# Attention and expert layer on one core: order of row maxima, low parts and pair products changed

## What is computed

```python
xn = _layernorm(x)
# attention: one head of 128, all 2048 keys for each query
qkv = xn @ w_qkv.T;  q, k, v = split(qkv)
probs = softmax((q @ k.T) * scale)             # needs the largest score of each row
attn = (probs @ v) reshaped @ w_proj.T + b_proj
# experts: 8 of them, each row goes to its best 2
h = xn @ W_in + b_in
route = top2 of softmax(h @ W_gate + b_gate), renormalised
mid = relu(h @ W1[e] + b1[e]);  eout = mid @ W2[e] + b2[e]
moe = (sum over e of route * eout) @ W_out + b_out
return x + attn + moe
```

## Time and profile before

| | us |
|---|---|
| median of 3 runs | 266.45 (265.16 to 271.34) |
| the profiled execution | 266.31 |
| its span, first to last instruction | 264.5 |
| TensorE busy | 233.3 (88%) |
| VectorE busy | 147.9 (56%) |
| GpSimd busy | 142.2 (54%) |
| ScalarE busy | 119.0 (45%) |
| mean granted clock of TensorE | 0.974 |

### The profile page before, as it was taken

How to read it: one execution, slowest core, us unless ns; L and a number is a source line. 1 busy time by engine, 2 the same in 40 slices (tenths; PEclk the granted TensorE clock), 3 DMA queues, 4 the chain that set the end, 5 groups by cost and what they waited for, 6 DMA issues and landing times.

```text
span 264.5 us, 4573 instructions
## 1 busy us (share of the span) xinstructions
PE 233.3 (88%) x1590; PEld 211.6 (80%) x1590; DVE 147.9 (56%) x340; ACT 119.0 (45%) x275; POOL 142.2 (54%) x163
## 2 busy tenths in 40 slices
PE   8898695978898888979999999999999489888994
PEld 8797594766686666779999999999988278788993
DVE  5945756277517867353545454545576535785462
ACT  1644240240264444733454545454477426546461
POOL 4029005888888810014666665656068888888300
PEclk9999898999999999999999999999999959999999
DMA  6799700111111021001222222222111113112011
GB/s 198 310 309 332 196 2 30 41 40 42 40 40 41 30 72 30 0 10 32 74 68 74 68 72 72 71 71 61 36 36 42 46 45 71 40 42 69 22 40 41
DMA packets 23047, 19.53 MB, mean 74 GB/s; under 512 B 3280, under 2 KB 19696, under 8 KB 22768
## 3 DMA queue, kind: packets, MB, share of 16 engines
q1 hardware_dynamic: 20000, 14.71, 18.5%
q0 software_dynamic: 2048, 4.20, 5.8%
q10 hardware_dynamic: 976, 0.33, 0.5%
HBM read 10.97 MB, written 8.26 MB: 73 GB/s over the span
## 4 chain that ended last, share of the span: by engine, by line
PE 67%; DVE 12%; POOL 6%; ACT 5%; issue 5%; DMA 3%; ACTq 1%; POOLq 0%; DVEq 0%
PE ps L1037 13%; PE ps L1023 13%; DVE part_max L598 7%; PE ps L848 5%; POOL wtab L380 5%; PE ps L789 4%; PE ps L791 4%; PE ps L790 4%; PE ps L910 3%; PE ps L797 3%; PE ps L923 3%; PE ps L919 3%; PE ps L920 3%; DMA w_raw<-in_L_attn_w_proj_dram 2%; ACT pf L455 2%
## 5 line engine op out<-in xcount | busy, mean ns | idle before, releaser
L343 POOL COPY wst<-wtab 128x1156 f32 x39 | 45.0, 1153 | 51.3 <-DVE y_sb L735 51.2
L608 DVE TENSOR_TENSOR pl<-pf,ph 128x512 fp32r<-128x512 f32 x48 | 35.2, 733 | 34.4 <-ACT pf L455 33.4
L455 ACT ACTIVATE pf<-ps 128x512 f32<-128x512 f32 x64 | 38.0, 594 | 28.9 <-PE ps L791 21.7
L454 ACT ACTIVATE ph<-ps 128x512 fp32r<-128x512 f32 x48 | 28.7, 599 | 38.6 <-PE ps L791 35.7
L598 DVE TENSOR_REDUCE part_max<-ps 128x1 f32<-128x1024 f32 x32 | 38.8, 1219 | 10.9 <-PE ps L848 8.6
L353 POOL DMA_INDIRECT slots_in<-hl,slots x32 | 32.8, 1024 | 21.8 <-DVE slots L674 14.8
L1037 PE MATMUL ps<-wst,mid 128*128 128x128 f32 x312 | 41.3, 275 | 0.9 <-DVE x_sb L625 0.9
L380 POOL DMA_INDIRECT wtab<-slots_out,slots x32 | 33.0, 1031 | 16.1 <-DMA slots_out<-y_sb 8.4
L1023 PE MATMUL ps<-xgT,wst 128*128 128x128 f32 x312 | 41.3, 275 | 0.0
L727 DVE TENSOR_SCALAR mid<-ps,wst 128x128 f32<-128x128 f32 x78 | 23.7, 346 | 28.9 <-PE ps L1023 28.9
L1037 PEld LDWEIGHTS ps<-wst,mid 128*128 128x128 f32 x312 | 38.0, 192 | 1.1 <-issue 1.0
(11 more groups left out here) (145 smaller groups left out, 359.0 us busy)
## 6 DMA issues: line engine op xcount, KB each, us to landing
wtab<-in_L_ffn_W_dram SPq DMA_DIRECT2D x16, 256.0 KB, 6.2
xg<-slots_in SPq DMA_DIRECT2D x39, 64.0 KB, 2.0
slots_out<-y_sb SPq DMA_DIRECT2D x39, 64.0 KB, 1.5
slots_in<-wst SPq DMA_DIRECT2D x2, 1024.0 KB, 5.0
x_sb<-in_L_attn_x_dram SPq DMA_DIRECT2D x4, 256.0 KB, 4.9
out_dram<-x_sb SPq DMA_DIRECT2D x3, 256.0 KB
wtab<-in_L_ffn_b_dram SPq DMA_DIRECT2D x1, 512.0 KB, 7.4
slots_in<-hl,slots POOLq DMA_INDIRECT x32
```

The costliest lines, as they stand in the source:

```text
L343: pool.tensor_copy(wst[:, t % 4, :], wtab[:, bass.ds(experts[t], 1), :].rearrange("p a n -> p (a n)")).then_inc(Z["staged"], 1)
L455: act.activation(pf[:, i % 3, :], ps[:, st_bank(i), :], ACT.Exp).then_inc(Z["pf_done"], 1)
L608: dve.tensor_tensor(pl[:, i % 3, :], pf[:, i % 3, :], raw(ph[:, i % 3, :]), ALU.subtract).then_inc(Z["lo_done"], 1)
```

## The change

The groups, the tiles and all instructions stay; what changes is their order on TensorE and VectorE.

1. VectorE takes the maxima of a step (and `row_max`) ahead of the step's low part, where it took them behind it.
2. Where a step has two pairs, TensorE makes the second behind `values`, where both stood ahead of it. If a step has one, it stays where it was.
3. The prefix product is issued in step 1 of the first group, not in step 3.
4. `PAIR_STEP` is spread anew for the second, third and fifth row: `[1, 2, 2, 3, 3, 4, 4, 5]` becomes `[1, 2, 2, 3, 4, 4, 5, 6]`, `[1, 2, 4, 5, 7, 8, 10, 11]` becomes `[1, 3, 5, 7, 9, 11, 12, 13]`, and `[1, 2, 3, 4]` becomes `[1, 2, 4, 5]`.
5. The second block of the experts' output is transposed at step 22 of phase two, not 21, and multiplied at 23. The counts that a transpose and a pair wait for are computed from the tables; they come to the same blocks and pairs as before.

```diff
-    PAIR_STEP = [[4, 5, 5, 6], [1, 2, 2, 3, 3, 4, 4, 5], [1, 2, 4, 5, 7, 8, 10, 11], [1, 4, 7, 10], [1, 2, 3, 4], []]
+    PAIR_STEP = [[4, 5, 5, 6], [1, 2, 2, 3, 4, 4, 5, 6], [1, 3, 5, 7, 9, 11, 12, 13], [1, 4, 7, 10], [1, 2, 4, 5], []]
...
-    BLOCK_AT = {12: 0, 21: 1, 25: 2}
+    BLOCK_AT = {12: 0, 22: 1, 25: 2}
...
             for g in range(PRE):
                 for k in range(STEPS[g]):
-                    if FIRST[g] + k >= PLAIN:
-                        low(FIRST[g] + k)
                     for m in pairs_at(g, k):
                         pair_max(g + 1, m)
                     if k == PAIR_STEP[g][-1]:
                         row_max(g + 1)
+                    if FIRST[g] + k >= PLAIN:
+                        low(FIRST[g] + k)
...
-                    low(i)
                     for m in pairs_at(g, k):
                         pair_max(g + 1, m)
                     if g + 1 < NG and k == PAIR_STEP[g][-1]:
                         row_max(g + 1)
+                    low(i)
...
-                for m in pairs_at(g, k):
-                    if m == 0:
-                        pe.wait_ge(Z["q_hi_ready"], g + 2)
-                    if g > PRE:
-                        pe.wait_ge(Z["moe_added"], 1)
-                    pair(g + 1, m)
+                for m in pairs_at(g, k)[:1]:
+                    step_pair(g, k, m)
+
+            def step_pair(g, k, m):
+
+                if m == 0:
+                    pe.wait_ge(Z["q_hi_ready"], g + 2)
+                blocks = sum(at < FIRST[g] + k - BASE_B for at in BLOCK_AT)
+                if g >= PRE and blocks > 0:
+                    pe.wait_ge(Z["moe_added"], blocks)
+                pair(g + 1, m)
...
-                    if g == 0 and k == 3:
+                    if g == 0 and k == 1:
                         prefix()
                     beside(g, k)
                     if i >= 2:
                         values(i - 2)
+                    for m in pairs_at(g, k)[1:]:
+                        step_pair(g, k, m)
```

More of the change, by code:

```diff
@@ L1061, in _, with moe_transpose @@
                 layer2(t)
-            def moe_transpose(b):
+            def moe_transpose(b, pairs):
                 pe.wait_ge(Z["c_ready"], TB * (b + 1))
-                if b == 0:
-                    pe.wait_ge(Z["max_read"], FIRST_PAIR[PRE + 2])
-                else:
-                    pe.wait_ge(Z["max_read"], FIRST_PAIR[NG])
+                pe.wait_ge(Z["max_read"], pairs)
                 for j in range(TB):
@@ L1092, in _ @@
                     if s in BLOCK_AT:
-                        moe_transpose(BLOCK_AT[s])
+                        moe_transpose(BLOCK_AT[s], FIRST_PAIR[g + 1] + sum(at <= k for at in PAIR_STEP[g]))
                     if s - 1 in BLOCK_AT:
@@ L1101, in _ @@
             values(LAST - 1)
-            moe_transpose(NR - 1)
+            moe_transpose(NR - 1, FIRST_PAIR[NG])
             for r in range(ROUNDS[NG - 1]):
```

## The result

| | before | after |
|---|---|---|
| median of the runs compared | 268.89 (265.16 to 271.36, 4) | 254.43 (253.91 to 255.89, 4) |
| profiled execution | 266.31 | 253.91 |
| its span | 264.5 | 252.2 |
| TensorE busy | 233.3 (88%) | 230.7 (91%) |
| mean granted clock | 0.974 | 0.986 |

The ratio is 0.957, 95% interval 0.951 to 0.963: faster. Forecast were 254.1 us, in a range of 251.0 to 258.8. Two of the four runs of the kernel before, 271.34 and 271.36, count as slow ones and are left out of the ratio, which therefore stands for some 11 us and not for the over 14 between the two medians. In the other comparisons its median was 266.3 to 266.7 us.

A forecast was written before the change was run, and what follows sets the result against it. Outside the expert stage, TensorE's pair matmuls waiting for VectorE's maxima (11 waits) were taken as the bound. Gains of 3.2 + 1.3 + 5.7 + 2.0 = 12.2 us off 266.31 gave 254.1 us, range 251.0 to 258.8.

The forecast's parts named there:

- Third group's stage: 75.11 to 109.20: four waits for maxima, costing 6.1 us with restarts, shrink to 0.4; gain 5.7 us (4.5 to 6.1).
- First group's stage: 39.51 to 50.18: earlier prefix product frees the maxima, gain 3.2 us (1.5 to 3.3), half of it a lower clock disappearing.
- Second group's stage: 53.94 to 75.11: the chain of eight maxima stays the bound; row product at 71.95, not 73.28, gain 1.3 us (0.5 to 1.6).
- The first maximum stays at 55.83: Second group's stage: its first maximum keeps its place, held by the query copy and the expert table.
- Expert stage: 109.20 to 189.00: untouched by the change, only starts earlier, near 99, with 4.6 us reserve before the first loaded rows.
- Behind it: Behind the expert stage: nothing until step 12, then the fifth group's waits of 2.7 us shrink to 0.6; gain 2.0 (1.0 to 2.6).
- first rival: The clock: idle pieces bring the lower level, 257.5 us, or shorter idle avoids it behind, 250.7; chance 0.12.
- The rule weighed: GpSimd table copies hold only low parts, never maxima, so 254.1 us stands; if maxima too, 1.4 us lost, 255.5.
- The low part as the late one: Third and fifth groups' stages: values wait for late low parts in every pair step, 14.6 us, 268.7 us; chance 0.04.
- no wait gone: Each wait moves to the next pair because reductions bound; only the prefix's 3.2 us remain, 263.1 us; chance 0.06.
- a gather as the gate: Behind step 12 GpSimd's gather sets the pace and the last 2.0 us go, 256.1 us; scatter or gather chance 0.08.
- clock rival: Lower clock in two stretches, 1.7 us each, 257.5 us; or at most 3.4 won between 207.70 and 224.08, 250.7; chance 0.12.

The follow-up runs named there:

- e1: The changed kernel with VectorE taking the low part of a step ahead of its maxima again, on the new table; 260.36 us, ratio 0.980.
- e5: The kernel before with one edit alone, maxima ahead of low parts in every step; 258.88 us, ratio 0.973.
- e6: The kernel before with one edit alone, the prefix product at step 1 of the first group; 263.93 us, ratio 0.994.
- e4: The changed kernel with the old tables, so pairs at their old steps and second block transposed at step 21; 256.53 us, ratio 0.961.
- e3: The changed kernel with both pairs of a step ahead of values again; 255.80 us, ratio 0.961.
- e11: e8 with GpSimd's four table copies behind scatters 6, 9, 12 and 15 instead of 20, 23, 26 and 29, without warming; 254.24 us, ratio 0.958.
- e8: The changed kernel with the expert table and gates taken in the first group's last step, not ahead of the second group's first maximum; 255.17 us, ratio 0.960.
- e2: The changed kernel with the prefix product back in step 3 of the first group; 257.26 us, ratio 0.967.
- e10: The changed kernel plus ten unread matmuls to keep TensorE warm in the wait before step 12's transposes; 253.96 us, ratio 0.956.
- e13: e12 with the first pair of the first group's steps one step earlier, at 3, 4, 5, 6; 251.71 us, ratio 0.948.
- e7: The changed kernel plus 30 unread matmuls to keep TensorE warm in the wait before step 12's transposes; 256.80 us, ratio 0.968.
- e12: e11 plus ten unread matmuls to keep TensorE warm in the wait before step 12's transposes; 252.39 us, ratio 0.950.

## Why the prediction was right

The time was right to 0.3 us, and the sum to 0.2 (12.2 forecast, 12.4 between the profiled executions). Not all of its terms were. The order of work accounts for some 9.9 of the 12.4: 1.7 in the first group's stage, 0.8 in the second, 5.4 in the third and 2.0 behind the expert stage. The other 2.5 are 1.6 and 1.2 us that the execution of before lost at the lower clock, less the 0.35 by which the changed kernel's first pair came later. The mechanism was right and gave four fifths of the forecast; that the sum came out to 0.2 is luck.

**Third group's stage: forecast 5.7, measured 5.39.** The mechanism is shown (e1, e5). The runs also separate what the prediction put together:

| first row product of the stage to expert transpose | low part first | maxima first |
|---|---|---|
| old table | 36.18 (before), 36.15 (e6) | 32.81 (e5, e4) |
| new table | 34.17 (e1) | 30.79 (after, e3) |

Order gives 3.4 with either table, the table 2.0 with either order; they add up, though the table's 2.0 are not the same waits: with low parts first they are two of the four stalls (e1 keeps 2.1 of 5.0), with maxima first the two waits behind held low parts that e4 shows. The 0.3 us between forecast and measurement is in the size of a stall. The forecast took 6.1 us for four of them, 0.28 each on top of the 5.0 of the rows, and let 0.4 stay. The 0.4 was right (0.3 at steps 12 and 13, above), so the four had cost 5.7, 0.17 each on top of the rows. e1 has 0.2: its piece is 3.4 longer with 2.7 in three waits.

**First group's stage: forecast 3.2, measured 3.35, and here the term was right by luck.** The step that failed is "half of this is the clock ... I take it as gone". The clock did go, but the change did not do it: e5 has the late prefix and the same idle pieces (1.47 and 1.32 us), and ran at 1.00 in 10.00 us. What the edit is worth is 10.00 - 8.29 = 1.7 us, near the forecast's lower bound of 1.5. The other 1.6 is shown for one execution of before. Its other runs differ in their clock too: of the 15 beside e5, five took 264.73 to 265.78 us at a mean granted clock of 0.980 or 0.981, and four took 265.85 to 266.74 at 0.974, which is also that of the profiled execution. So the forecast started from an execution of the second sort. Where in the span the other runs had the lower clock, their means don't tell. The 0.35 us by which the changed kernel's first pair comes later lie in code that the sum did not look at; with it the scatter began 1.9 us earlier (39.8, before 41.7), not 2.3.

**Second group's stage: forecast 1.3, measured 0.8.** "The first maximum stays at 55.83" failed in part. It moved with the row product, as meant, but its distance from it grew from 55.83 - 49.99 = 5.84 to 53.17 - 46.99 = 6.18. The last work ahead of it is the expert table, after and before:

```profile
52.80 0.46 DVE L680 TENSOR_SCALAR texp<-texp_f 128x40 int32<-128x40 f32 x1
53.17 1.21 DVE L598 TENSOR_REDUCE part_max<-ps 128x1 f32<-128x1024 f32 x1
```

```profile
55.73 0.18 DVE L680 TENSOR_SCALAR texp<-texp_f 128x40 int32<-128x40 f32 x1
55.83 1.22 DVE L598 TENSOR_REDUCE part_max<-ps 128x1 f32<-128x1024 f32 x1
```

The conversion took 0.28 longer, and that is most of the 0.34; it stood beside an addition of GpSimd (52.72 to 53.19), before beside an indirect DMA. It does not come with the change: e5 and e6, whose second group is that of before, have a distance of 6.12 and 6.11, and e1, whose second group is the changed one, has 5.87. From there to the row product it took 16.32, where the forecast has 16.12. The waits for maxima came down to 2.1 and not to 3. Of the rest of the term, e3 and e4 show the parts: with both pairs ahead and the old table it is 23.3 to 23.6 (before, e5, e6), with one of the two edits 22.9 (e3) and 22.7 (e4), with both 22.5. Against e5 and e6 (23.6 both) the term is 1.1 and not 0.8, nearer to the forecast.

**Expert stage: forecast unchanged, 79.8, beginning near 99.** It took 79.79 and began at 100.02, 9.2 earlier instead of 10.2; the missing 1.0 is the sum of the errors above (0.35 + 0.5 + 0.3 - 0.15). The first loads were no gate: no wait of TensorE in this stretch names them.

**Behind it: forecast 2.0, measured 3.21.** From the first pair of the fifth group's stage to the end it is 40.46 before and 38.41 after, so 2.0 as forecast. It is all order: 38.59 in e5 and 38.63 in e4 with the old table (and the second block's transposes at their old step, so that this move cost nothing either), 40.89 in e1 with the new one. The prediction let the table do part of it ("from 2 to 4 there are over 3 us"); it does none. The other 1.2 lie in the stretch from the transposes to that pair:

```profile
203.23:213.74 10.51, 10.51 (x53) 9.22 (x54) 4.20 (x8) 5.47 (x11) 9.00 (x10) 0.84 0.22 62
```

Before, it is

```profile
212.41:224.08 11.67, 11.67 (x54) 10.19 (x54) 4.43 (x8) 5.46 (x11) 9.83 (x11) 0.75 0.29 61
```

TensorE is busy in all of both; they differ by the clock. At 1.00 the stretch takes 8.9 us, and it did so in e5, e11 and all four kernels with calls to keep warm, while the other eight profiles have 10.2 to 11.7. The idle time ahead of it doesn't sort them: with 4.7 us of it the stretch took 10.2, 10.4 and 11.7, with 3.7 to 3.8 it took 8.9 twice and 10.5 to 11.6 five times. So it isn't shown that the change brought the 1.2. The prediction named this in its first rival as up to 3.4 to be won, and kept it out of the sum. So 1.2 from a clock that I had left out made good the 1.0 that the stages ahead fell short. A low part that is late for its values, because a maximum now stands ahead of it, is there once, 0.62 us at 195.08, in the stage where the wait of 3.78 us follows and covers it, as forecast.

**The rule weighed.** Rows and rule agree: a copy holds low parts (two of them for 2.59 us above, one for 1.88 in e4, and one for 1.69 in e8), and no reduction in this profile is over 1.226 us. This is what the Trainium skill, "SBUF — State Buffer", section "Who interferes with whom", states for a VectorE instruction with two SBUF inputs beside a GpSimd one that reads SBUF. For the changed kernel "254.1 stands" held, since no wait of its third stage stands behind a copy. But I had looked only at the values that read the held part. What was late in e4 was what stood behind it on VectorE, a maximum and `scale_out` (2.0 us); in e2 and e8 it was `scale_out` and, with two low parts in 2.76, the values product after all (0.85). Whether it costs anything turned on a shift of a microsecond or two between TensorE and the copies. With maxima first, the table's 2.0 us are this protection as far as e4's trace goes: both its waits stand behind a held low part. e4 was not run with the copies moved, which would show it.

**Rivals.** The low part as the late one (268.7) and no wait gone (263.1) did not come: the waits for maxima fell from 13.9 to 3.2 us, and L923 waits 0.6 in all; a gather as the gate (256.1) did not come, though with the fast clock behind step 12 the stage behind it was 0.35 to 0.8 longer in e10 to e13 (38.8 to 39.2, to the end), but not in e5 and e7 (38.6 and 38.5), for which I have no cause shown. Of the clock rival, the gain side came in part (1.2 of at most 3.4), the loss side not.

## What to carry to other kernels

On an engine that works in order, put the result that another engine's next work waits for ahead of one that is needed steps later, and then space the waits by more than the cycle (here 2.05 us), so that a held instruction finds room. Before you book a stretch at a lower clock to the change, ask whether the same code would run at the full clock in another execution; a kernel that differs elsewhere tells. And if a gain in one stage returns as a loss in the next, look for what kept its place in time while the rest moved.

## What the runs showed of the hardware

- **The clock of the same code differs between executions.** The code ahead of the first pair is the same on TensorE but for the prefix product. Leaving out e13, whose first pair was moved, the pair stands at 38.4 to 38.8 us in the six profiles with a mean clock of 0.96 ahead of it, at 39.5 to 39.8 in four with 0.91, and at 40.88 and 40.71 in e10 and e11 with 0.92 (0.70 in the last 4.7 us of it in e10). e7 had 1.00 there and its pair at 38.76, so that the lower clock of the first six cost nothing: where it falls decides the price.
- **Matmuls in an idle time kept the clock up.** Behind the idle time of step 12 (3.7 to 4.7 us) the stretch had 1.00 in two of the ten profiles without calls to keep warm and in all four with them. e12 and e11 differ only in the ten calls, and all runs of e12 have a higher mean clock (0.990 at least against 0.986 at most) and a shorter time. With e10 against the changed kernel the gain was 0.5 us with overlapping runs, so the size of the gain isn't settled.
- **Keeping warm has a price of its own.** A 128x128 matmul in plain float32 takes two passes, 0.113 us each at the full clock. Ten calls (20 passes, some 2.3 us) fit in a wait of 3.8 us, thirty do not.
- **A copy of 1.16 us by GpSimd can hold a two-input VectorE instruction of 0.69 us for 1.0 to 1.5 us more**, up to 2.164 us in all (e2), while a reduction from PSUM beside it stays at 1.226.
